# A fused cross-attention and mixture-of-experts kernel: projections moved into the fill, and new orders on four engines

## The reference: what is computed

```python
# stage 1: cross-attention on the layer-normed rows
q = einsum('oc,bct->bot', Wq, layernorm(x)) + bq
k = einsum('oc,bct->bot', Wk, ctx) + bk          # v likewise, with Wv, bv
scores = einsum('bhkt,bhks->bhts', q, k) * 16 ** -0.5
out = einsum('bhts,bhks->bhkt', softmax(scores), v)
x = x + einsum('oc,bct->bot', Wo, out) + bo
# stage 2: 2048 tokens of 512, 8 experts, 2 chosen per token, one shared expert
h = rmsnorm(layernorm(x)) * w
probs = softmax(h @ router_w); topv, topi = top_k(probs, 2); topv /= sum(topv)
moe = sum over the chosen experts of topv * ((silu(h @ Wg[e]) * (h @ Wu[e])) @ Wd[e])
x = x + moe + (silu(h @ sg) * (h @ su)) @ sd
```

## Time and profile before

| | us |
|---|---|
| runs | 834.0 median of 3 (829.28 to 836.18) |
| the profiled execution | 831.6, its span from first to last instruction 829.9 |
| granted TensorE clock, mean | 0.989 of full speed |
| start of the fill's first pass | 28.37 |
| first `scores` of half 0 | 53.38 |
| barrier to the token stage | about 507 |
| first product of the block loop | 603.36 |
| last product of the block loop | about 816 |

### The profile page before, as it was taken

How to read it: one execution, slowest core, us unless ns; L and a number is a source line. 1 busy time by engine, 2 the same in 40 slices (tenths; PEclk the granted TensorE clock), 3 DMA queues, 4 the chain that set the end, 5 groups by cost and what they waited for, 6 DMA issues and landing times. The chain is left out here.

```text
span 829.9 us, 11858 instructions
## 1 busy us (share of the span) xinstructions
PE 782.5 (94%) x3877; PEld 395.3 (48%) x3877; DVE 548.2 (66%) x1048; ACT 419.4 (51%) x800; POOL 363.6 (44%) x309
## 2 busy tenths in 40 slices
PE   7999999999999999999999999998989999999993
PEld 3434334434334343343333455775445666666662
DVE  5787888898888888878888767777643233322331
ACT  2115666767767777677776674310333233333331
POOL 4207427317328155182222421000127777777774
PEclk9999999999999999999999999999999999999997
DMA  8957476566565765667543235511925666666663
GB/s 282 217 116 195 98 161 144 111 133 154 136 139 120 169 153 111 146 133 152 131 83 121 93 104 216 216 51 38 360 70 97 98 100 102 100 94 99 98 100 44
DMA packets 54186, 109.67 MB, mean 132 GB/s; under 512 B 12200, under 2 KB 27304, under 8 KB 49888
## 3 DMA queue, kind: packets, MB, share of 16 engines
q1 hardware_dynamic: 37080, 79.39, 38.4%
q0 software_dynamic: 16960, 29.37, 19.0%
q10 hardware_dynamic: 88, 0.16, 0.1%
HBM read 67.90 MB, written 40.86 MB: 131 GB/s over the span
## 5 line engine op out<-in xcount | busy, mean ns | idle before, releaser
L1061 DVE TENSOR_REDUCE negmax<-front_ps 128x1 f32<-128x512 f32 x512 | 326.7, 685 | 69.2 <-PE front_ps L911 67.4
L811 ACT ACTIVATE probs<-st_ps 128x512 f32<-128x512 f32 x512 | 284.6, 598 | 151.8 <-PE st_ps L945 135.0
L1340 POOL DMA_INDIRECT out<-ring,row_i x78 | 122.5, 1571 | 66.5 <-ACT ring L1393 50.6
L1564 PE MATMUL big_ps<-w_gu,attn 128*128 x244 | 113.0, 601 | 3.5 <-ACT attn L1386 3.5
L648 POOL CAST early<-early 128x512 fp32r<-128x512 f32 x28 | 17.1, 610 | 165.9 <-ACT early L764 165.9
L1773 DVE TENSOR_TENSOR zeros<-attn,big_ps 128x256 f32<-128x256 f32 x39 | 16.4, 421 | 83.0 <-ACT attn L1405 83.0
L945 PE MATMUL st_ps<-stacks 50*128 50x512 f32 x256 | 68.5, 493 | 2.2 <-ACT probs L811 1.9
L1405 ACT ACTIVATE attn<-big_ps 128x256 f32<-128x256 f32 x39 | 15.0, 384 | 109.8 <-PE big_ps L1564 109.8
L1323 POOL DMA_INDIRECT ring<-h_rows,row_i x39 | 39.5, 1014 | 68.2 <-DMA out<-x_sb 56.6
L958 PE MATMUL pv_ps<-probs,v_t 128*32 128x512 f32 x512 | 68.2, 605 | 0.5 <-ACT probs L811 0.5
L958 PE MATMUL pv_ps<-probs,early 128*32 128x512 f32 x512 | 68.2, 605 | 0.3
(11 more groups left out here) (212 smaller groups left out, 1219.3 us busy)
## 6 DMA issues: line engine op xcount, KB each, us to landing
parts_dram<-early SPq DMA_DIRECT2D x32, 512.0 KB, 4.4
stacks<-parts_dram SPq DMA_DIRECT2D x32, 256.0 KB, 5.4
w_gu<-in_gate_up SPq DMA_DIRECT2D x8, 1024.0 KB, 12.7
x_sb<-in_x SPq DMA_DIRECT2D x8, 512.0 KB, 9.7
early<-in_ctx POOLq DMA_DIRECT2D x8, 512.0 KB, 5.5
stacks<-parts_dram SPq DMA_DIRECT2D x32, 128.0 KB, 6.1
k_stack<-parts_dram SPq DMA_DIRECT2D x16, 256.0 KB, 4.6
q_stack<-parts_dram SPq DMA_DIRECT2D x16, 256.0 KB, 5.3
```

Of the source, the lines that this page charges most:

```text
L811: nc.scalar.activation(probs[:, k % 2, u % GH, :], score_bank(UNITS * s + u), ACT.Exp, scale=SCALE).then_inc(exp_done, 1)
L1061: nc.vector.tensor_reduce(negmax[:, n % 2, c:c + 1], smax_bank(UNITS * n + u), AX_X, ALU.max, negate=True).then_inc(max_done, 1)
L1340: nc.gpsimd.indirect_dma_start(outs[i], bass.IndirectOffsetOnAxis(ap=row_i[:, k:k + 1], axis=0), y_sb[:, k % RING, DY * i:DY * (i + 1)], N ...
L1564: mm = nc.tensor.matmul(gu_ps[:, :], h_t[:, k % 2, a, :], w_gu[:, bass.ds(expert, 1), a, :], start=(a == 0), stop=(a == DT - 1))
```

## The change

1. **Fill.** `FIRST` is 4: K and Q of half 3 and both calls of the values of batch 1 are projected in the fill, in eight of the places in which products on zeros stood. The values go to two banks of `st_ps`, which is not in use before the first `scores`. Half 0 no longer projects anything (`projected(0)` and `value_batch(0)` are None); in its first eight pairs stand products on zeros instead, of 512 columns in the first four and 256 in the next four. ScalarE's bias additions and copies and SyncE's DMAs move with them.
2. **Half 1.** Its four products on zeros have 256 columns instead of 512.
3. **Statistics.** In halves 3 to 14 `row_stats_of` stands one pair after the residual it belongs to, instead of right behind it.
4. **Half 14.** The fourth product on zeros stands at u = 16 instead of 14; the 12 BN_AGGR are cut in two groups of 6, and the Newton steps stand one pair later. Two products on zeros of 256 columns follow the last `pv`.
5. **Token stage.** The gate groups of j = 2 and the logits of the last four row tiles alternate; the count products stand between the two gate groups of j = 3, and `shared_down(2)`, `shared_down(3)` behind them; on VectorE `shared_add(2)`, `shared_add(3)` and `shared_act(3)` move some instructions back.
6. **Before the loop.** On ScalarE the copy `turn_in(0)` stands ahead of the high parts of experts 6 and 7.

```diff
-FIRST = 3
+FIRST = 4
+LATE = 2
-        FIRST_UNITS = (2, 4, 8, 10)
+        FIRST_UNITS = ((2, 4), (8, 10), (12, 14), (22, 24))
+        VALUE_UNITS = ((6, 16), (20, 26))
+        def projected(s):
+            return s + 3 if 0 < s and s + 3 < HALVES else None
...
@@ SyncE, the fill
+                for i in range(2):
+                    load_stack(LATE + 1, i)
                 load_x(4, B)
...
@@ ScalarE, the fill
+                qk_bias(3, 0)
+                v_copy(1, 0)
                 rows_half_out(act, 0)
                 rows_half_in(act, 0, first_loaded)
+                qk_bias(3, 1)
+                v_copy(1, 1)
...
@@ TensorE, project_qk
+                        if n == 3:
+                            pe.wait_ge(qk32_ready, 2 * n)
+                        if n == 3:
+                            pe.wait_ge(nm_parts_ready, 1)
...
@@ TensorE, the fill and the halves
+                    i, kts = halves_at(FIRST_UNITS, u)
+                    r, tiles = halves_at(VALUE_UNITS, u)
+                    if kts:
+                        project_qk(LATE + i // 2, i % 2, kts)
+                    elif tiles:
+                        project_v(1, r, tiles)
                     else:
                         filler(pv_ps[:, 0:FILL])
...
-                        if s == 0 and u == 0:
-                            filler(pv_ps[:, :])
+                        if s == 0 and u < HALF_UNITS:
+                            pe.wait_ge(nm_parts_ready, 2)
+                            filler(proj_ps[:, 0:T if u < HALF_UNITS // 2 else F])
                         if s == 1 and u in (18, 22, 26, 30):
-                            filler(proj_ps[:, :])
-                        if s == HALVES - 2 and u in (2, 6, 10, 14):
+                            filler(proj_ps[:, 0:F])
+                        if s == HALVES - 2 and u in (2, 6, 10, 16):
...
@@ VectorE
                             residual(dve, out_batch(s), ended_at(late_units(s), u), proj_ps[:, :])
-                            row_stats_of(out_batch(s), ended_at(late_units(s), u))
+                            if s == HALVES - 1:
+                                row_stats_of(out_batch(s), ended_at(late_units(s), u))
+                        if s < HALVES - 1 and out_batch(s) is not None and ended_at(late_units(s), u - 2) is not None:
+                            row_stats_of(out_batch(s), ended_at(late_units(s), u - 2))
...
@@ ScalarE, before the loop
-                for e in range(E):
+                for e in range(KEPT):
+                    down_high_part(e)
                 turn_in(0)
+                for e in range(KEPT, E):
+                    down_high_part(e)
...
@@ TensorE, token stage
-                shared_gates(2, (0,))
-                for t in range(EARLY, NTILE):
-                    logits(pe, t)
-                shared_gates(2, (1,))
-                for t in range(GT):
-                    shared_down(t)
+                for i in range(CT):
+                    shared_gates(2, (i,))
+                    for t in range(EARLY + CT * i, EARLY + CT * (i + 1)):
+                        logits(pe, t)
+                shared_down(0)
+                shared_down(1)
+                shared_gates(3, (0,))
                 pe.wait_ge(chosen_ready, 1)
...
-                shared_gates(3)
+                shared_gates(3, (1,))
+                shared_down(2)
+                shared_down(3)
```

More of the change, by code:

```diff
@@ L303, in value_batch @@
         def value_batch(s):
-            return s // 2 + 1 if s % 2 == 0 and s // 2 + 1 < B else None
+            return s // 2 + 1 if s % 2 == 0 and 0 < s and s // 2 + 1 < B else None
+        def projected(s):
+            return s + 3 if 0 < s and s + 3 < HALVES else None
         def maxima_until(s, u):
@@ L409, in row_stats, with row_variance @@
             chained(dve, last)
-        def row_variance(dve, lo, hi, scale=1.0, eps=LN_EPS):
-            for t in range(lo, hi):
+        def row_variance(dve, lo, hi, scale=1.0, eps=LN_EPS, first=None):
+            for t in range(lo if first is None else first, hi):
                 last = nc.vector.bn_aggr(mv[:, t, :], stats[:, t, :])
@@ L767, in v_copy @@
                 def v_copy(b, r):
+                    from_bank = st_ps[:, 1 + r, :] if b == 1 else proj_ps[:, :]
                     act.wait_ge(v_ready, 2 * b + r + 1)
@@ L879, in project_v @@
                     if 0 in tiles:
-                        if r == 1:
+                        if b == 1:
+                            pe.wait_ge(bo_ready, 1)
+                            pe.wait_ge(x1_ready, X1_START)
+                        elif r == 1:
                             pe.wait_ge(vt_copied, 2 * b + 1)
@@ L889, in project_v @@
                             pe.wait_ge(w_split, 2)
-                        here, there = slice(st * P, (st + 1) * P), proj_ps[:, C * i:C * (i + 1)]
+                        bank = st_ps[:, 1 + r, :] if b == 1 else proj_ps[:, :]
+                        here, there = slice(st * P, (st + 1) * P), bank[:, C * i:C * (i + 1)]
                         for kt in range(CT):
@@ L1007, in _ @@
                         i, kts = halves_at(kq_units(s), u)
-                        if s + 3 < HALVES and kts:
+                        if projected(s) is not None and kts:
                             project_qk(s + 3, i, kts)
@@ L1036, in _ @@
                 pv(STEPS * HALVES - 1)
+                for _ in range(2):
+                    nc.tensor.matmul(st_ps[:, 0, 0:F], zeros[:, 0:P], zeros[:, 0:F], start=True, stop=True)
             @block.vector
@@ L1124, in _ @@
                             residual(dve, out_batch(s - 1), 1, proj_ps[:, :])
+                        if u == 2 and spread(s - 1) and out_batch(s - 1) is not None:
                             row_stats_of(out_batch(s - 1), 1)
@@ L1657, in _ @@
                 run = src
+                shared_add(2)
+                shared_add(3)
                 total = run[:, NTILE - 1, :]
@@ L1679, in _ @@
                 chained(dve, V.tensor_tensor(POS, POS, cnt_ps[:, 0, :, :], ALU.add))
+                shared_act(3)
                 for c, m in enumerate((M1, M2)):
```

42 lines of the change are left out of this document (21 added, 21 removed).

## The result

The changed kernel takes 825.43 us, median of 10 executions (822.15 to 827.22), beside 834.61 for the kernel before, median of 10 (829.28 to 841.22). The ratio is 0.9879, 95% interval 0.9857 to 0.9901. The prediction was 825.0. That the prediction lies so close is partly chance, as the profile shows: the profiled execution of after took 826.63 (span 824.8), only 5.0 less than the 831.6 that was profiled before.

The account below looks back on a forecast made before the run. TensorE, busy 94% of the span, was taken as the bound; +1.7 - 2.3 - 1.3 - 2.1 - 0.8 + 0.5 - 4.7 = -9.0 us turned the median 834.0 into 825.0. The forecast reached from 821.5 to 828.5, eight in ten from 819 to 831.

Parts of the forecast that it names:

- Fill: Stretch before the first scores: four K or Q pieces, four value tiles and two new waits, less 0.4 slack: +1.7 us.
- Half 0: Attention half 0: four projections go (-7.7), products on zeros come (+5.2), short pairs give 0.2 back: -2.3 us.
- half 1: Attention half 1: four products on zeros lose half their columns, the first worth nothing behind a wait: -1.3 us.
- Statistics: Halves 3 to 13: statistics one pair later shorten TensorE's waits for reduces, -1.2 and -0.9: -2.1 us.
- half 14: Half 14: the fourth product on zeros no longer waits 0.98 for the split maxima: -0.8 us.
- Token front: Token stage's start: last logits follow a second gate group, routing starts later, adds move: +0.5 us, between -0.7 and +2.8.
- Ahead of the loop: Before the block loop: earlier ScalarE copy cuts TensorE's 3.53 wait (-2.9) and avoids the clock's fall (-1.8): -4.7 us.
- (a): Rival: it goes better, fill costs 1.0, half 1 gives 2.1, token front gains 0.7: 822.3 us, chance 0.14.
- (b): Rival: the clock falls ahead of the block loop all the same: 826.8 us, chance 0.10.
- (d): Rival: VectorE's new orders, statistics and half 14, do nothing: 827.9 us, chance 0.05.
- (c): Rival: VectorE becomes the bound in the fill and first halves, turning the shorter list into waits: 828.0 us, chance 0.12.
- (e): Rival: slower, the removed zeros had kept the clock up in half 0's first eight pairs and half 1: 843, chance 0.05.

Follow-up runs that it names:

- gate kernel: The changed kernel with the first gate group of j = 7 ahead of the wait for the places instead of behind it: 825.12 us, ratio 0.9872.

## Why the prediction was right, and where not

- **Fill, +1.7:** +2.3. The waits were sized right, and the 0.4 that was let go did come back: the second wait stands where 0.43 was lost before. Mis-sized was the tile of values: 1.06 from start to start where a product on zeros took 0.84, so +0.9 for the four and not +0.3. This term is the whole difference of 0.6.
- **Half 0, -2.3, and half 1, -1.3:** -1.7 and -0.9. The products of 256 columns cost 0.63, not 0.5, which is 0.5 of half 0's missing 0.6. In one short pair the reduces bind (1.34 for 0.63), but before, two groups had waited 0.3 each. In half 1 the first wait grew from 0.30 to 0.72, as foreseen, and one of 0.34 came behind the third product. The three terms give -0.3, for -1.9 forecast; measured alone, ratio 0.9990 [0.9964, 1.0016].
- **Statistics, -2.1, and half 14, -0.8:** the waits went as forecast in halves 5 to 14 (0.8, 0.6 and 0.6 in the first pair of profiles), but half 3 got 0.5 to 1.0 longer wherever one of its Newton steps was held by GpSimd, which the sum had not thought of. By the rows -1.5 in the first pair, between -1.4 and -2.5 in the others. Measured alone -4.0 (-5.7 to -2.3): the missing part was clock. The falls in halves 13 and 14 cost 0.95, 3.7 and 2.1 in three of the five old-order profiles, 1.35 on the mean over the five. Rows and falls together give about -2.9 for the first pair.
- **End zeros, 0:** +0.4 by the profile, nothing that the totals show.
- **Token front, +0.5:** right as a length, 64.84 for 64.37, wrong as a worth. Over the five profiles with the old order the stretch took 64.4, 65.9, 65.9, 67.5 and 67.5, mean 66.2; the new one takes 64.8 to 65.0. That is -1.4, and -1.4 is what the medians of this part alone gave.
- **Ahead of the loop, -4.7:** -2.8 and -1.7 by the profile, -3.8 (-6.0 to -1.6) measured alone. Right, with its reasoning on the clock: the fall came in five of five with the long wait and never with 0.77.

These worths, rows and falls together, add up to -0.3 - 2.9 + 0.4 - 1.4 - 4.5 = -8.7 of the 9.2 measured.

Against the profiled execution the sum was not right: it said 822.6, and 826.63 came, and the first product of the loop stood at 598.93 and not near 596.2. Of these 4.0, 1.6 are the fill and halves 0 and 1, 1.4 the statistics and half 14, 0.4 the end zeros and 0.2 the stretch ahead of the loop; single blocks of the loop took 1.2 more, and the first pass began 0.8 earlier. The medians hide this, since the profiled execution of before lay 3.0 below its kernel's median and that of after 1.2 above.

So the total was right by two errors that met. The step that failed is the one in which all sums are "made against the profiled execution" and then "I add the difference to the median": it took the falls of that one execution as those of the kernel. The trace of before had two; the mean clock of the executions says that there are more. From before to after it rose from 0.986 to 0.9925, which at half speed is 0.013 of 830 us or some 11 us less at the lower level (about 1 of them in the idle end of the program, where it costs nothing); at 1.5 to 1.7 us for 3.4 that is 4 to 5 of the 9.2, where the prediction had 1.8. Against that, the fill, half 0 and half 1 brought 1.6 less than forecast. Times and mean clocks of single executions say the same: over the 35 of the kernel before, 0.001 of mean clock goes with 0.8 us (correlation -0.86), and over the 23 on another chip with 0.6 (-0.73), so that 0.0065 is worth 4 to 5. Where in each execution the falls lie is not known, for only one of each kernel has a trace; and the 0.986 and the 0.9925 were not measured side by side.

Of the rivals, (a), (b) and (d) fell. (c) was right in its direction: the sizes of the fill and of halves 0 and 1 came out 1.6 to its side, where it gave 3.0. (e) didn't come as a whole, but its mechanism is real: without half 0's zeros the kernel loses some 10 us, and half 1, which lost half of its columns, has falls that it did not have. The forecast's reason against it, that the clock was 1.00 before, was no evidence for a shorter list, since in the trace of before four projections and a product on zeros stood in those pairs. And the forecast's reach of 821.5 to 828.5 does not follow from its bounds: added up, they give 821.2 to 836.0.

## What to carry to other kernels

Where single executions differ by more than a change is worth, compare their mean clock with that of the profiled one before making a sum against it. A short wait is worth its length plus the chance of a fall behind it, here mostly 1.5 to 1.7 us each: 0.75 us was followed by one in some executions and not in others, with the same rows ahead. Take a product on zeros out only after a profile of several executions without it, and best one by one: without the last four of the eight here half 0 got 1.25 shorter and the clock stayed up, without all eight the kernel lost some 10 us. Before moving small VectorE instructions, look at what GpSimd does at that time.

## What was not expected of the hardware

- In half 0 without the zeros the clock stayed at its lower level for 54.6 us with TensorE busy 53.6 of 54.0 us. What keeps it low there was not tried apart; the first-pass and second-pass products read only 48 or 50 rows.
- 32 products of 8 columns in a row were followed by a fall in four of five profiles, without idle time ahead of it (in the one shown TensorE was busy 5.00 of 5.00 us).
- A VectorE TENSOR_TENSOR of 8 columns took 1.22 instead of 0.16, until GpSimd's TENSOR_TENSOR ended; in the changed kernel one took 0.89 in the same way (172.96 to 173.85, GpSimd's 172.55 to 173.83), and in the gate kernel a SCALAR_TENSOR_TENSOR 1.28 (175.17 to 176.45, GpSimd's 175.15 to 176.43). The reduces beside them, which read PSUM, kept their 0.6. The Trainium skill, "SBUF — State Buffer", section "SBUF: two separate sides", has it that a VectorE operation with two SBUF inputs and a GpSimd operation share one pair of ports as an exclusive lock for the whole instruction; the trace agrees, to 0.02 us.
